# A message-passing layer on one core: one table for both projections, x and result in blocks of 500 columns, the range count moved late, b2 by a float32r diagonal

## The reference

```python
h = relu(layernorm(x))                      # x: 12500 nodes x 48
x_i, x_j = h[dst], h[src]                   # 400000 edges, sorted by dst
z = concat([x_i, x_j, edge_attr], 1) @ W1 + b1   # (48 + 48 + 32) -> 128
msg = relu(z) @ W2 + b2                     # 128 -> 48
out = x + segment_sum(msg, dst, 12500)
# src = randint(0, 12500); dst = int(12500 * u**2), u uniform in [0, 1), then sorted
```

## Time and profile before

| | us |
|---|---|
| median of three runs (3543.72, 3558.9, 3557.3) | 3557.3 |
| the profiled execution's own time | 3545.33 |
| its span, first to last instruction | 3543.5 |

### The profile page before, as it was taken

How to read it: one execution, slowest core, us unless ns; L and a number is a source line. 1 busy time by engine, 2 the same in 40 slices (tenths; PEclk the granted TensorE clock), 3 DMA queues, 4 the chain that set the end, 5 groups by cost and what they waited for, 6 DMA issues and landing times.

```text
span 3543.5 us, 90188 instructions
## 1 busy us (share of the span) xinstructions
PE 3362.3 (95%) x22072; PEld 2944.4 (83%) x22072; DVE 2587.7 (73%) x6230; ACT 1749.6 (49%) x5837; POOL 2675.9 (76%) x2808
## 2 busy tenths in 40 slices
PE   7799999999999999999999999999999999999998
PEld 6788888888888888888888888888888888888887
DVE  8677777777777777777777777777777777777774
ACT  5355555544444454444454544444544444544443
POOL 8777777777777777777777777777777777777776
PEclk9999999999999999999999999999999999999997
DMA  9533333433333333333333333333333333333334
GB/s 282 116 110 105 105 105 106 109 101 101 99 103 104 99 100 101 103 102 101 99 101 104 100 101 101 100 104 99 101 100 101 104 100 99 101 101 103 101 100 100
DMA packets 269474, 378.34 MB, mean 107 GB/s; under 512 B 86612, under 2 KB 150789, under 8 KB 268310
## 3 DMA queue, kind: packets, MB, share of 16 engines
q0 software_dynamic: 89344, 180.86, 20.6%
q1 hardware_dynamic: 179622, 194.55, 18.7%
q10 hardware_dynamic: 464, 2.43, 0.4%
HBM read 360.48 MB, written 17.02 MB: 107 GB/s over the span
## 4 chain that ended last, share of the span: by engine, by line
PE 43%; POOL 27%; issue 18%; DMA 7%; ACT 2%; DVE 2%; POOLq 0%; ACTq 0%; SPq 0%; DVEq 0%
POOL gath L459 27%; PE ps L1119 19%; PE ps L1103 9%; PE ps L1095 8%; DMA gath<-b_table,idx 7%; PE ps L1152 2%; PE ps L1109 1%; DVE gath L832 1%; PE ps L1069 1%; ACT gath L564 1%; PE ps L1110 1%; ACT work L574 1%; PE ps L1144 1%; PE ps L1159 0%; ACT idx L548 0%
## 5 line engine op out<-in xcount | busy, mean ns | idle before, releaser
L459 POOL DMA_INDIRECT gath<-b_table,idx x2736 | 2603.3, 951 | 838.3 <-issue 785.6
L1119 PE MATMUL ps<-h_tab,p_hot 128*128 128x480 f32 x6720 | 1682.9, 397 | 0.0
L1119 PEld LDWEIGHTS ps<-h_tab,p_hot 128*128 128x128 f32 x6720 | 1246.6, 194 | 178.1
L574 ACT ACTIVATE work<-ps,work 128x96 f32<-128x96 f32 x3360 | 848.8, 344 | 540.0 <-PE ps L1119 534.1
L564 ACT ACTIVATE gath<-gath 128x512 f32<-128x512 f32 x684 | 431.8, 631 | 1094.5 <-DVE gath L832 1088.1
L1103 PEld LDWEIGHTS ps<-onehot,gath 128*128 128x128 f32 x5472 | 689.1, 194 | 254.3 <-ACT gath L564 213.5
L832 DVE TENSOR_TENSOR gath<-ps,gath 128x512 f32<-128x512 f32 x684 | 473.0, 691 | 577.4 <-DMA gath<-b_table,idx 566.3
L1103 PE MATMUL ps<-onehot,gath 128*128 128x48 f32 x5472 | 738.7, 279 | 139.5 <-ACT gath L564 136.4
L1095 PE MATMUL ps<-rhs,lhs 96*128 96x128 f32 x5472 | 791.9, 289 | 12.9 <-DVE lhs L824 12.9
L1095 PEld LDWEIGHTS ps<-rhs,lhs 96*128 96x128 f32 x5472 | 688.5, 197 | 13.0 <-issue 13.0
L824 DVE TENSOR_SCALAR_CACHE_REDUCE lhs<-nodes 48x512 f32<-48x512 f32 x684 | 508.8, 744 | 35.7 <-issue 8.9
(11 more groups left out here) (106 smaller groups left out, 1612.5 us busy)
## 6 DMA issues: line engine op xcount, KB each, us to landing
nodes<-dst_row SPq DMA_DIRECT2D x782, 96.0 KB
lhs<-in_edge_t SPq DMA_DIRECT2D x684, 64.0 KB
gath<-b_table,idx POOLq DMA_INDIRECT x2736
work<-key_row SPq DMA_DIRECT2D x84, 256.0 KB, 3.7
rhs<-a_table SPq DMA_DIRECT2D x684, 24.0 KB
work<-in_edge_t SPq DMA_DIRECT2D x196, 32.0 KB
b_table<-nodes SPq DMA_DIRECT2D x7, 512.0 KB, 4.2
a_table<-nodes SPq DMA_DIRECT2D x7, 512.0 KB, 5.6
```

The costliest lines, as they stand in the source:

```text
L459: pool.indirect_dma_start(gath[:, u, t, :], None, b_table, bass.IndirectOffsetOnAxis(ap=idx[:, u, t:t + 1], axis=0)).then_inc(gathered[u], 16)
L574: m = nc.scalar.activation(p_sel[:, t % 2, RUN_COLS * q + j, :], ps_run[:, r % 2, j * split:(j + 1) * split], ACT.Copy, scale=p_mask[:, RU ...
L1119: mm = nc.tensor.matmul(ps_run[:, r % 2, :].rearrange("p (j w) -> p j w", j=RUN_COLS), p_hot[:, t % 2, i, :], h_parts[:, first:first + BLO ...
```

## The change

One DRAM table `ab_table` holds for node n row 2n (A) and row 2n + 1 (B), each 512 bytes. The two stores per piece become one, of rows of 1024 bytes (14 DMAs in place of 28). Indices are doubled once on VectorE (`2 * src + 1`, 3072 columns, ahead of `find_rel`), the boundaries `part_from` of the picked groups are doubled, and the first index copies on ScalarE move from within the last chunk to behind the loop. `a_table` becomes a view of every second row.

x and the result are laid out in DRAM as 25 blocks of 48 x 500. The five loads take 5 blocks each, rows of 2000 bytes in place of 10000. `front` is 24 blocks (12000 columns), stored in four pieces of 6 blocks; the last block is stored after the last addition. `store_front` is called after the last cycle's loads, no longer among them.

The range count runs in four quarters in the cycle before the last; its sum, `flag` and `settled` come in the last cycle. What waited for `flag` at the main stage's start no longer does.

The fold's b2 term: ScalarE scales the identity by the degrees, in place of b2; TensorE multiplies b2, split into a high and a low float32r part, by that diagonal, in two float32r products.

```diff
-    front = n_nodes * 95 // 100
-    pieces = 5
+    front_blocks, front_pieces, pieces = blocks - 1, 4, 5
+    front = front_blocks * block_cols
...
-    a_table = nc.dram_tensor("a_table", [padded, hidden], F32).ap()
-    b_table = nc.dram_tensor("b_table", [padded, hidden], F32).ap()
+    ab_table = nc.dram_tensor("ab_table", [2 * padded, hidden], F32).ap()
...
-                    sp.dma_start(b_rows[:, j0:j1, :], ab_stage[:, c % 2, 2 * u0:2 * u1, 1, :]
-                                 ).then_inc(b_stored[k][c % 2], 16)
-                    sp.dma_start(a_rows[:, j0:j1, :], ab_stage[:, c % 2, 2 * u0:2 * u1, 0, :]
-                                 ).then_inc(a_stored[k][c % 2], 16)
+                    sp.dma_start(ab_rows[:, j0:j1, :],
+                                 ab_stage[:, c % 2, 2 * u0:2 * u1, :, :].rearrange("p j t h -> p j (t h)")
+                                 ).then_inc(ab_stored[k][c % 2], 16)
...
-                    if final and j >= 3:
-                        store_front(j - 3)
...
             cycle(cycles - 1, 0, final=True, more=False)
+            for k in range(front_pieces):
+                store_front(k)
...
-            sp.dma_start(out_t[:, front:n_nodes], out_sb[:, front:n_nodes]).then_inc(out_stored, 16)
+            sp.dma_start(out_t_blocks[:, front_blocks:blocks, :], out_blocks[:, front_blocks:blocks, :]).then_inc(out_stored, 16)
             front_settled = sp.value_load(settled[0:1, 0:1], min_val=0, max_val=1)
             with sp.If(front_settled < 1):
-                for k in range(pieces):
+                for k in range(front_pieces):
                     part = slice(k * front_piece, (k + 1) * front_piece)
-                    sp.dma_start(out_t[:, part], out_sb[:, part]).then_inc(out_stored, 16)
+                    sp.dma_start(out_t_blocks[:, part, :], out_blocks[:, part, :]).then_inc(out_stored, 16)
...
             def load_x(k):
-                act.dma_start(out_sb[:, k * piece:(k + 1) * piece], x_t[:, k * piece:(k + 1) * piece]).then_inc(xt_in, 16)
+                part = slice(k * piece, (k + 1) * piece)
+                act.dma_start(out_blocks[:, part, :], x_blocks[:, part, :]).then_inc(xt_in, 16)
...
-                nc.scalar.activation(b2_deg[r:r + WIN, k // 2 % 2, :], b2_bc[0:WIN, :], ACT.Copy, scale=deg[:, u:u + 1]
-                                     ).then_inc(b2_ready, 1)
+                nc.scalar.activation(deg_diag[r:r + WIN, k // 2 % 2, k % 2 * WIN:(k % 2 + 1) * WIN],
+                                     ident[0:WIN, 0:WIN], ACT.Copy,
+                                     scale=deg[:, u:u + 1]).then_inc(b2_ready, 1)
...
+            dve.wait_ge(src_in, 32)
+            nc.vector.tensor_scalar(src_sb[:, early_tiles:n_tiles], src_sb[:, early_tiles:n_tiles], 2.0, 1.0,
+                                    ALU.mult, ALU.add).then_inc(src_doubled, 1)
             find_rel()
+            dve.wait_ge(b2_hi_ready, 1)
+            nc.vector.tensor_tensor(b2_two[:, 1, :], b2_bc[:], b2_two[:, 0, :].bitcast(F32), ALU.subtract
+                                    ).then_inc(b2_lo_ready, 1)
...
+                    if c == cycles - 2 and j % 2 == 0:
+                        count_inside(j // 2)
+                    if final and j == 3:
+                        judge()
...
-                nc.tensor.matmul(ps_out, b2_deg[:, k // 2 % 2, :], pair_ident[:], start=False, stop=True
-                                 ).then_inc(folded, 1)
+                for h in range(2):
+                    mm = nc.tensor.matmul(ps_out, b2_two[0:e_row + WIN, h, :], deg_diag[:, k // 2 % 2, :], start=False, stop=(h == 1))
+                mm.then_inc(folded, 1)
```

More of the change, by code:

```diff
@@ L32, in gnn @@
 def gnn(nc, x_rows, x_main, x_last, x_t, src_t, src_p, dst_t, dst_n, edge_t, w1, b1, w2, b2, out_t):
-    feat, n_nodes = x_t.shape
+    blocks, feat, block_cols = x_t.shape
+    n_nodes = blocks * block_cols
     edge_feat, edge_cols = edge_t.shape
@@ L59, in gnn @@
     late_groups = late + 2
-    front = n_nodes * 95 // 100
-    pieces = 5
-    piece, front_piece = n_nodes // pieces, front // pieces
+    front_blocks, front_pieces, pieces = blocks - 1, 4, 5
+    front = front_blocks * block_cols
+    piece, front_piece = blocks // pieces, front_blocks // front_pieces
     gen_cols, gen_k = 500, 5
@@ L69, in gnn @@
     assert PERIOD == 2 * SLOTS and LEAD == SLOTS and early_tiles == EARLY_A + EARLY_B
-    assert rounds * gen_cols * gen_k == n_nodes and piece * pieces == n_nodes and front_piece * pieces == front
-    a_table = nc.dram_tensor("a_table", [padded, hidden], F32).ap()
-    b_table = nc.dram_tensor("b_table", [padded, hidden], F32).ap()
+    assert rounds * gen_cols * gen_k == n_nodes and piece * pieces == blocks and front_piece * front_pieces == front_blocks
+    ab_table = nc.dram_tensor("ab_table", [2 * padded, hidden], F32).ap()
     dst_row = nc.dram_tensor("dst_row", [P, n_tiles], F32).ap()
@@ L213, in gnn @@
         prod_ready, ab_ready = sem("prod_ready"), sem("ab_ready")
-        b_stored = [[sem(f"b_stored{k}_{b}") for b in range(2)] for k in range(len(stores))]
-        a_stored = [[sem(f"a_stored{k}_{b}") for b in range(2)] for k in range(len(stores))]
+        ab_stored = [[sem(f"ab_stored{k}_{b}") for b in range(2)] for k in range(len(stores))]
         idx_ready, hot_ready, hott_ready = sem("idx_ready"), sem("hot_ready"), sem("hott_ready")
@@ L524, in _ @@
                     take_ab(c, u)
-                    if c == chunks - 1 and u == 0:
-                        act.wait_ge(src_in, 32)
-                        for s in range(SLOTS):
-                            nc.scalar.copy(idx[:, s, :], src_sb[:, (EARLY + s) * TILES:(EARLY + s + 1) * TILES]
-                                           ).then_inc(idx_ready, 1)
             act.wait_ge(iota_ready, 5)
@@ L1158, in fold_tail @@
                 nc.tensor.matmul(ps_out_p, w2_sb[:], sums_p[:], start=True, stop=False)
-                nc.tensor.matmul(ps_out_p, p_b2_deg[e_row:e_row + WIN, :], ident[e_row:e_row + WIN, e_row:e_row + WIN],
-                                 start=False, stop=True).then_inc(p_folded, 1)
+                for h in range(2):
+                    mm = nc.tensor.matmul(ps_out_p, b2_two[0:e_row + WIN, h, :], p_deg_diag[0:e_row + WIN, :],
+                                          start=False, stop=(h == 1))
+                mm.then_inc(p_folded, 1)
             def cycle(c, it, first=False, final=False):
@@ L1179, in cycle @@
                         turn_e(c, it)
+                    if final and j == 2:
+                        pe.wait_ge(inside_step, 8)
+                        pe.wait_ge(p_picked, items * runs)
+                        nc.tensor.matmul(ps_cov, ones_col[:], covered[:], start=True, stop=True).then_inc(cov_summed, 1)
                     if not final:
@@ L1255, in layouts @@
         x,
-        x[:main].reshape(-1, P, x.shape[1]).transpose(1, 0, 2), x[main:], x.T,
+        x[:main].reshape(-1, P, x.shape[1]).transpose(1, 0, 2), x[main:], x.T.reshape(x.shape[1], -1, X_COLS).transpose(1, 0, 2),
         src.reshape(-1, P).T, own.reshape(P, -1), dst.reshape(-1, P).T, dst.reshape(P, -1), edge.T,
@@ L1274 @@
     r = run_bass_kernel_spmd(nc, [arrays], core_ids=[0])
-    return np.ascontiguousarray(r.results[0]["out_t"].T)
+    out = r.results[0]["out_t"]
+    return np.ascontiguousarray(out.transpose(0, 2, 1).reshape(-1, out.shape[1]))
```

114 lines of the change are left out of this document (63 added, 51 removed).

## The result

The changed kernel takes 3572.64 us (median of 8 runs, 3566.76 to 3575.18), the kernel before in the same series 3557.24 us (median of 8, 3543.72 to 3562.08). The ratio is 1.0045, with a 95% interval of 1.0031 to 1.0058: 15.4 us slower, between 11 and 21. The forecast was 3563, in a range of 3547 to 3576. The profiled execution is one at the slow end of its kernel, 3575.18 us with a span of 3573.3, and the one of before lies near the fast end, 3545.33 with 3543.5. So their spans differ by 29.8 us where the medians differ by 15.4. Cut at the first gather, at gather 300 of 2736 and at the last one, the 29.8 are -2.7, then +4.5, +12.6 and, behind the last gather, +15.4. (Gather 300 begins at 475.50 us, before at 473.69.)

A forecast was written before the change was run, and what follows sets the result against it. GpSimd's back-to-back gathers were taken to bound the kernel. Start and x -2.5, steady 0, last fold -0.2 and drain +14.4 gave +11.7, which on a middle of 3551.3 made 3563 us, range 3547 to 3576.

The forecast's parts named there:

- Result stores: End of kernel: settled becomes 0, so four front stores go out after the last addition; +14.4 us.
- Rival 4: Final stores: drain at the low rate, 129 GB/s, +17.7; with nearly no start gain +16.4 in all, 3568 us; chance 0.14.
- rival 3: Final stores: drain at half of full width, 197 GB/s, 11.7 us; +8.8 in all, 3560 us; chance 0.11.
- Start and x: Start and first loads of x: earlier gathers and smaller stalls, 2.5 us saved, between 1.1 and 7.
- at least 1.1 us (x moves 1.1 earlier, everything else stays): Start and loads of x: the least gain, with x's loads 1.1 us earlier and all else unchanged.
- rival 6: Main stage: TensorE waits more, its clock drops, late sums hold gathers up; once, +16.7, 3568 us; chance 0.03.
- Rival 1: Start: gathers get through beside x and tables, both stalls end; -7 for -2.5, +7.2 in all, 3558 us; chance 0.15.
- Rival 2: Loads of x: short rows change nothing for gathers, which wait as long; -1.1 alone, +13.1 in all, 3564 us; chance 0.16.
- Steady stage: Main stage: gathers keep their pace, 80 per 100 us, and the moved range count costs nothing; 0 us.
- b2 by a float32r diagonal: Folds: two float32r products save 30 us of TensorE time, worth nothing to the end except about 0.2 in the last fold.
- busy TensorE some tens of us lower: Whole kernel: a sign that was to show the forecast right, TensorE's busy time falling by some tens of us.
- Tables: Start: table stores in rows of 1 KB take 5 us less, between 0 and 11; worth 2 us to early gathers.

The follow-up runs named there:

- e2: The changed kernel with late = 14 and x loaded in rows of 10000 bytes again; 4919.44 us, 1.0022 of the kernel before on a slower core.
- e6: Repeat of the changed kernel with late = 14 and x in rows of 10000 bytes; 4924.11 us, 1.007 of the kernel before.
- e1: The changed kernel with late = 14 in place of 16, so settled is 1 again; 4920.58 us, 1.0026 of the kernel before.
- e5: Repeat of the changed kernel with late = 14, short rows of x kept; 4924.67 us, 1.0047 of the kernel before.
- e10: Another repeat of the changed kernel with late = 14, short rows of x kept; 4879.53 us, 0.9993 of the kernel before.
- e12: The last repeat of the changed kernel with late = 14, short rows of x kept; 4897.71 us, 1.0039 of the kernel before.
- e7: The kernel before with x alone loaded in rows of 2000 bytes; 4902.1 us, 1.0005 of the kernel before.
- e4: The kernel before run again, nothing changed; 4899.11 us, ratio 0.9987.
- e9: The changed kernel run again, nothing further changed; 4908.96 us, 1.0024 of the kernel before.

## Why the prediction was right, and where it was off

**Result stores, +14.4: right, and the whole of the result.** `settled` is 0, the block's store is followed by the four after 1.08 us (predicted 1.02), and they take 16.5 us to the last landing (predicted 1.24 + 14.6 = 15.8). The piece behind the last gather's start grew from 12.6 to 28.0 us, by 15.4 for a predicted 14.4 - 0.2 = 14.2. With the threshold alone in the kernel before, the 17.3 us are there; with `late = 14` they are gone, in four runs of four. The choice of x's 158 GB/s as the price was near: it was 140. Rival 4 (129 GB/s, +17.7) was 2 us off, rival 3 (197, +8.8 in all) is out. The stretches have 169, 175 and then 113 GB/s, at engine shares of 0.78, 0.87 and 0.64: the last third goes at a lower share of the engines, which no term had. The Trainium skill (SBUF — State Buffer, section "Door 1: The DMA port swizzle") puts the limit for partitions 0 to 63 at about 218 GB/s. By that rule the trace agrees as an upper bound: no 5 us reach it.

**Start and x, -2.5: the mis-sized term.** It was made up of 2 us for the tables and of a gain at x's stalls, and it measures +1.8 at gather 300 (475.50 us for 473.69). The first part held: the first gather is 2.7 us earlier, and x's loads 2.2 (predicted 1.1). The step that failed is "at least 1.1 us (x moves 1.1 earlier, everything else stays)". Everything else did not stay. In short rows the gather gets through 2.9 us earlier behind x's first load, and x's own transfer is slower, 15.2 us to landing in the median for 13.9, so the first addition gained 0.7 of x's 2.2. And there is now a stall for x, in front of the fold: TensorE, which has run out of work behind VectorE, comes back at the lower level of its clock a second time (at 128.55, shown above), where the kernel before had gone through that once, ahead of the first addition. The second addition slips by 3.2 us. The clock between the two additions of the profile after and of the profile before:

```profile
126.70:136.61 9.91, 8.06 (x33) 7.03 (x34) 5.37 (x12) 3.38 (x12) 3.78 (x4) 0.66 0.15 40
```

```profile
127.43:134.00 6.57, 6.57 (x38) 5.41 (x37) 5.38 (x12) 3.13 (x11) 3.81 (x5) 0.90 0.47 109
```

That clock was rival 6's mechanism, in a place where the prediction had not looked for it. That the row length sets off both the wait and the clock in the changed kernel is shown by e2 and e6 against e1, e5, e10 and e12. In e7, with the short rows in the kernel before, the wait came and the granted clock between the additions was 0.91. The trace shows why: TensorE did not stand there. First e7, then `e10_late14`:

```profile
168.60 4.35 PE L1120 MATMUL ps<-h_tab,p_hot 128*128 128x480 f32 x10
...
172.78 1.12 PE L1104 MATMUL ps<-onehot,gath 128*128 128x48 f32 x8
```

```profile
174.99 1.94 PE L1120 MATMUL ps<-onehot,gath 128*128 128x48 f32 x8 [6.48 <-ACT gath L568]
```

Pauses before earlier products had put off its work in e7 until x was there; in e10 it stood for 6.48 us. Yet e7's second addition comes 11.3 us behind the first, later than in any run with the low clock, after a wait of 4.86 us whose cause the profile doesn't tell. So the clock accounts for the slip in the changed kernel (the same 33 products, 2.85 us dearer), and not for every slip on these cores.

Rival 1 had the first half (the third group's wait 6.44 to 3.65), and not its gain. Rival 2 is out: the row length did change when the gathers came in. The Trainium skill (DMA: Bandwidth & Descriptors, section "Queues, rings and completion order") has an engine drain a whole packet of many descriptors from one queue before the next. If a packet holds a number of rows, rows five times shorter make its turn shorter, and by that rule, the trace agrees; rival 2 had taken all the rows that an engine has of a load as one turn. No run told the two readings apart.

**Steady stage, 0: right for the count, and not the whole of the profile's difference.** 80 gathers per 100 us stayed. Yet 12.6 us of the 29.8 lie between gather 300 and the last. One gather and pause is 1.252 us in the median for 1.249, which over 2436 is 7.3 us, and the rest are longer single ones (101 over 1 us from gather 301 on, before 71). Is that the change? The step is not: it is 1.252 in the kernel before run again (e4) and in e2, e5 and e7, and 1.249 in the changed kernel run again (e9) and in e1, e10 and e12. One kernel has both. The mean duration of a gather in the four `late = 14` runs, one kernel, is 952, 952, 952 and 954 ns (2604.0 to 2609.4 us in all), 951 to 953 in three runs of the kernel before or with one edit of it. So part of it comes and goes between executions. The 956 of the profile after is above all of these, and what made the single ones longer stays open. The medians of 8 runs differ by 15.4, which is the drain (+15.4) with nearly nothing left for the start's 1.8 and for this; the interval leaves 5 us either way.

**b2 by a float32r diagonal, 30 us of TensorE saved: 13.5**, 113.8 to 100.3, 684 records as before: the end of the bounds at which records stay, with the record 18 ns shorter. It was priced at nothing for the time. No run where gathers bound the time tests that; the last fold has 0.40 us for 0.53. The sign "busy TensorE some tens of us lower" did not come: its products are 3370.8 us busy in all, for 3362.3, at a mean clock of 0.971 for 0.975.

**Tables, 5 us off:** a store of both tables (1024 KB) lands in 5.0 us in the median, where A's (512 KB), behind B's, took 5.6. The first gather begins at 87.89, at the early edge of the 88 to 90 that were to show it. VectorE did wait for b2's high part, 6.87 us (80.56, predicted "about 81.4"). That was to be covered by the last early rows, and was not wholly:

```profile
89.99 0.65 DVE L702 TENSOR_REDUCE key_sb<-gath 128x10 f32<-128x480 f32 x1
```

Before, VectorE waited for these rows, and took them up 2.43 us behind the start of their last gather (89.38 to 91.81). Now that gather starts at 86.64, so by that distance they are there at about 89.1, an estimate, and VectorE comes 0.9 us late. That is part of why x gained 2.2 us and the gathers 2.7.

**The median.** 3563 was built on the middle of two levels, 3551.3; five more runs of the kernel before put its median at 3557.2, which is what the median of the first three, 3557.3, had said. On that ground the forecast would have been 3557.2 + 11.7 = 3569. Of the 9.6 us by which it was low, 5.9 lay in the base and 3.7 in the sum, where the profiles show 4.3 for the start and 1.2 for the drain; the difference is within the interval. Both errors had one sign, and the time lies within the range because its upper end, 3576, was built on the upper runs.

No version of this kernel was shown to be faster than the one before. On a core bound by gathers, `late = 14` with long rows of x should take back both losses. That is argued from the pieces. The same kernel on the slower cores (e2, e6) had ratios of 1.0022 and 1.007 and bears no gain out.

## What to carry to other kernels

A threshold that decides whether work may be hidden has a value in the data: compute it, as here 11941 against 11875 and 12000, before moving the threshold. Output that leaves behind the last computation costs its full transfer, so what matters is that stores are left over; here four of short rows and five of long ones cost nearly the same (16.5 and 15.9 us). Shorter rows in one load let another queue's transfers through, but the load itself then lands later; ask which of the two the next wait hangs on.

## What the runs showed of the hardware

- A store of 2.304 MB from 48 partitions with nothing beside it took 16.5 us (140 GB/s) in four pieces of 2000-byte rows. In five pieces of 9600-byte rows (2.304 MB too) it took 15.9: the last issue at 4905.7 and 9.3 us to landing, from 4899.1. Row length makes little difference there: 0.6 us, with the number of pieces changed too.
- The same program takes 3557 us on one core and about 4900 on others, with the gathers at 951 and 952 ns in both, and with 326.4 us of unexplained pauses of TensorE before z's products where the fast core has none. Its granted clock over the span is 0.84 to 0.86 there and 0.97 in the profile after. What differs was not found.
- Where VectorE stood 6 to 9 us for one late load, the granted clock between the next two additions was 0.55 to 0.66 in seven profiles of eight, and TensorE had stood for 3.5 to 6.5 us just before: 7.76 us at 0.58 for products that take 4.91 at 1.00. In the eighth (e7, 0.91) TensorE had work until the load was there.
- The step from gather to gather, 1.249 or 1.252 us in the median, differs between executions of one kernel; over 2436 gathers that is 7.3 us.
